# Graph attention: one-hot matrices of edges by one VectorE compare per step, six PSUM banks for the sums, and a reordered seam between edge stage and node stage

## What is computed

```
def _gat_layer(x, src, dst, W, a_src, a_dst, b, heads, concat):
    n = x.shape[0]
    h = (x @ W).reshape(n, heads, -1)
    al_s = jnp.einsum('nhf,hf->nh', h, a_src)
    al_d = jnp.einsum('nhf,hf->nh', h, a_dst)
    e = jax.nn.leaky_relu(al_s[src] + al_d[dst], NEG_SLOPE)
    m = jax.lax.stop_gradient(jax.ops.segment_max(e, dst, num_segments=n))
    ex = jnp.exp(e - m[dst])
    denom = jax.ops.segment_sum(ex, dst, num_segments=n)
    alpha = ex / (denom[dst] + 1e-16)
    out = jax.ops.segment_sum(h[src] * alpha[:, :, None], dst, num_segments=n)
    out = out.reshape(n, -1) if concat else out.mean(axis=1)
    return out + b
```

## Time and profile before

| | before |
|---|---|
| median of 3 timed runs | 7338.19 us (7330.99 to 7347.03) |
| the profiled execution | 7389.03 us |
| its span in the trace | 7387.3 us |
| mean granted TensorE clock | 0.754 |
| TensorE busy | 4888.9 us, 66% |
| VectorE busy | 4342.4 us, 59% |
| GpSimd busy | 3668.7 us, 50% |
| ScalarE busy | 2620.5 us, 35% |

### The profile page before, as it was taken

How to read it: one execution, slowest core, us unless ns; L and a number is a source line. 1 busy time by engine, 2 the same in 40 slices (tenths; PEclk the granted TensorE clock), 3 DMA queues, 4 the chain that set the end, 5 groups by cost and what they waited for, 6 DMA issues and landing times. The chain is left out here.

```text
span 7387.3 us, 99572 instructions
## 1 busy us (share of the span) xinstructions
PE 4888.9 (66%) x21954; PEld 3578.6 (48%) x21954; DVE 4342.4 (59%) x12539; ACT 2620.5 (35%) x7524; POOL 3668.7 (50%) x3680
## 2 busy tenths in 40 slices
PE   5666699996666666666666667466666666666662
PEld 4455488885444444444444445344444444444441
DVE  8999776665455555545555558444444454544447
ACT  6774222221444444444444445222222222222221
POOL 1333311112566666666666653566666666666660
PEclk8887799997666767676777779676667776777676
DMA  8999644333343434343444334333333333333336
GB/s 341 378 390 384 244 126 136 110 110 96 107 116 111 116 112 115 111 114 112 116 111 115 111 101 132 108 110 111 106 110 105 109 105 111 105 110 105 110 110 224
DMA packets 384742, 1062.90 MB, mean 144 GB/s; under 512 B 103698, under 2 KB 195782, under 8 KB 359382
## 3 DMA queue, kind: packets, MB, share of 16 engines
q0 software_dynamic: 168928, 459.50, 23.4%
q1 hardware_dynamic: 206902, 549.39, 20.5%
q10 hardware_dynamic: 8640, 51.39, 1.7%
HBM read 795.11 MB, written 264.87 MB: 143 GB/s over the span
## 5 line engine op out<-in xcount | busy, mean ns | idle before, releaser
L259 POOL DMA_INDIRECT rows<-table_d,idx x3328 | 3215.4, 966 | 2095.4 <-issue 801.6
L307 PE MATMUL pG<-rows,onehot 128*128 128x264 f32 (+1 forms) x6656 | 2568.1, 537 | 934.0 <-issue 660.3
L510 DVE TENSOR_TENSOR acc<-acc,pG 128x264 f32 (+1 forms) x3328 | 1413.8, 425 | 1898.8 <-remote 743.0
L307 PEld LDWEIGHTS pG<-rows,onehot 128*128 128x128 f32 x6656 | 1625.9, 264 | 1516.2 <-issue 885.5
L371 ACT ACTIVATE onehot<-pQ 128x1024 f32<-128x1024 f32 (+1 forms) x512 | 439.7, 859 | 2515.0 <-DMA pre_in<-pre_d 1347.5
L378 ACT ACTIVATE rows<-rows 128x64 f32<-128x64 f32 (+1 forms) x4480 | 1255.4, 367 | 26.9 <-issue 22.4
L938 PE MATMUL pH<-hT_pre,w1h 128*128 128x256 f32 x1568 | 470.5, 466 | 188.6 <-ACT hT_pre L799 150.0
L938 PEld LDWEIGHTS pH<-hT_pre,w1h 128*128 128x128 f32 x1568 | 366.0, 240 | 277.2 <-ACT hT_pre L799 166.4
L1075 DVE SCALAR_TENSOR_TENSOR run<-run,same_e,ea 128x96 f32<-128x96 f32 x1567 | 488.5, 312 | 7.2 <-DMA ea<-in_ea 6.3
L1075 DVE SCALAR_TENSOR_TENSOR run<-run,cut_e,ea 128x96 f32<-128x96 f32 x1567 | 488.3, 312 | 0.0
L492 DVE TENSOR_TENSOR rows<-rows,pA 128x1024 f32<-128x1024 f32 x384 | 466.9, 1216 | 4.4
(11 more groups left out here) (295 smaller groups left out, 4560.5 us busy)
## 6 DMA issues: line engine op xcount, KB each, us to landing
rows_d<-run SPq DMA_DIRECT2D x98, 1536.0 KB
onehotT<-drow_d SPq DMA_DIRECT2D x128, 832.0 KB
ea<-in_ea SPq DMA_DIRECT2D x98, 768.0 KB
rows<-table_d,idx POOLq DMA_INDIRECT x3328
pre_d<-pre ACTq DMA_DIRECT2D x49, 1024.0 KB
pre_in<-pre_d SPq DMA_DIRECT2D x49, 1024.0 KB, 5.1
hrow_c<-table_d SPq DMA_DIRECT2D x98, 256.0 KB
tab<-tab_d SPq DMA_DIRECT2D x64, 260.0 KB
```

Source lines behind the costliest of these rows:

```text
L259: g.indirect_dma_start(out=rows[:, at.par, k, 0:XF + H], out_offset=None, in_=table, in_offset=bass.IndirectOffsetOnAxis(ap=idx[:, at.par, ...
L307: mm = pe.matmul(pG[(k + 2 * at.par) % 4][:, 0:W], onehot[:, k, :], rows[:, at.par, k, :], start=True, stop=True)
L510: v.tensor_tensor(to, to, pG[(k + 2 * at.par) % 4][:, 0:W], ALU.add).then_inc(added, 1)
```

## The change

In attention, `spans`, `hots`, the tiles drow and pQ, the loads of drow and the semaphores between them are gone. In their place `edge_hots` on VectorE compares a row of 128 numbers (`keep["iota"]`) with a table of each edge's place in its node tile (`keep["near"]`, 128 x 1664 in bf16, made once in `node_mlp` and kept in SBUF): one instruction per step for 26 items, in the order late items of b, early items of b+1. The aggregates have six banks instead of four. ScalarE weighs the late items in one run. The DRAM array drow has one row instead of five.

At the seam, the places where runs begin are computed between groups of edges (`heads_of_runs`, three groups behind `ROW_AT`); the last group's run is stored in two halves; the scatter is awaited by GpSimd at the start of `node_mlp`; the weights have semaphores of their own, those of attention are issued by ScalarE; TensorE waits only for w1, and `project_attention` stands behind step 0 and step 16. The item tables lose some VectorE operations, and a third list (near, 13 tiles) is transposed in steps 14 to 17.

```
 attention
+            def edge_hots(b, first=False, chain=True):
+                w = EARLY if first else TB if chain else TB - EARLY
+                near = keep["near"][:, 0:w] if first else keep["near"][:, bass.ds(b.n * TB + EARLY, w)]
+                i = TB - w if first else 0
+                v.tensor_tensor(onehot[:, i:i + w, :], keep["iota"][:, :].unsqueeze(1).to_broadcast([P, w, P]),
+                                near.unsqueeze(2).to_broadcast([P, w, P]), ALU.is_equal).then_inc(edges_hot, 1)
...
             def step(b, first=False, chain=True, ahead=True, after=True):
                 n = b.plus(1)
+                edge_hots(b, first, chain)
                 if not first:
                     late = node_tiles(nc, v, jrow_v, b, EARLY, TB)
...
             def aggregate(at, ks):
                 for k in ks:
-                    if k % QT == 0:
-                        pe.wait_ge(near_used, near_at(at, k // QT) + 1)
+                    if k == 0:
+                        pe.wait_ge(edges_hot, at.n + 1)
+                    if k == EARLY:
+                        pe.wait_ge(edges_hot, at.n + 2)
...
                     if k % 2 == 0:
-                        pe.wait_ge(added, at.n * TB + (k + 2))
-                    mm = pe.matmul(pG[(k + 2 * at.par) % 4][:, 0:W], onehot[:, k, :], rows[:, at.par, k, :],
+                        bank_read = k - BANKS + 2 if k >= BANKS else k - BANKS if k else 0
+                        pe.wait_ge(added, at.n * TB + (BANKS + bank_read))
+                    mm = pe.matmul(pG[k % BANKS][:, 0:W], onehot[:, (k - EARLY) % TB, :], rows[:, at.par, k, :],
                                    start=True, stop=True)
...
                 part(EARLY, 16)
-                spans(n, 0, first)
...
-                spans(n, 2)
                 if ahead:
                     destinations(m, tiles)
-                aggregate(n, range(0, 8))
-                spans(n, 3)
-                aggregate(n, range(8, EARLY))
+                aggregate(n, range(0, EARLY))
...
-                hots(n, 0)
-                hots(n, 1)
...
-                weigh(n, range(EARLY, 16))
-                hots(n, 2)
-                weigh(n, range(16, 20))
-                hots(n, 3)
-                weigh(n, range(20, TB))
+                weigh(n, range(EARLY, TB))
...
-                if after:
-                    sp.wait_ge(near_ready, near_at(n, NQ - 1) + 1)
-                    load_drow(o)
...
 edge_chains, node_mlp
-        assert ROW_AT < NG and PAIR == 2 and EW <= ET
+        HEADS_AT = ROW_AT + 3
+        assert HEADS_AT < NG and PAIR == 2 and EW <= ET
...
+                if g == HEADS_AT:
+                    heads_of_runs()
...
-            g.wait_ge(fix_out, 16)
...
+            g.wait_ge(keep["fix_out"], 16)
             all_steps(g, step, first=0)
...
-            pe.wait_ge(w_in, 16 * 10)
-            pe.wait_ge(projected, 1)
+            pe.wait_ge(w1_in, 16 * 5)
...
-            v.wait_ge(w_in, 16 * 10)
-            project_attention(v, chain, wg, att, tmp, H)
-            v.sem_inc(projected, 1)
...
                 if n == 0:
-                    v.wait_ge(late_in, 16 * 4)
+                    v.wait_ge(wg_in, 16 * 3)
+                    project_attention(v, chain, wg, att, tmp, H)
+                    v.sem_inc(projected, 1)
+                if n == 16:
+                    v.wait_ge(late_in, 16 * 3)
                     project_attention(v, chain, wg2, att2, tmp, 1)
```

More of the change, by code:

```diff
@@ L117, in attention @@
     D = XF // H
-    QT = 8
-    CHUNKS = [range(q, min(q + QT, TB)) for q in range(0, TB, QT)]
-    NQ = len(CHUNKS)
     EARLY = 12
+    BANKS = 6
     DG = EARLY // 4
@@ L241, in _ @@
             load_jv(one)
-            sp.wait_ge(blank, 1)
-            load_drow(one)
-            load_drow(two)
             load_jpe(two)
@@ L272, in _ @@
         def _(pe):
-            def spans(at, q, first=False):
-                if q == 0:
-                    pe.wait_ge(drow_in[at.par], at.fills * 16 + 16)
-                if not first:
-                    pe.wait_ge(near_used, near_at(at, q))
-                for k in CHUNKS[q]:
-                    mm = pe.matmul(pQ[:, k - q * QT, :], drow[:, at.par, k, :], keep["nrow"][:, :],
-                                   start=True, stop=True, skip_group_check=True)
-                mm.then_inc(near_ready, 1)
             def destinations(at, tiles):
@@ L1040, in tile_row, with heads_of_runs @@
                 done(v.tensor_copy(keep["jT"][:, :], pU[1][0:KT, 0:P]))
+            def heads_of_runs():
+                v.wait_ge(counted, 2)
+                v.scalar_tensor_tensor(out=place[:, 1:EW], in0=same[:, 1:EW], scalar=float(EW), in1=count_i[:, 1:EW],
+                                       op0=ALU.mult, op1=ALU.add).then_inc(masked, 1)
+                v.wait_ge(masked, 6)
+                v.memset(place[:, 0:1], float(EW)).then_inc(masked, 1)
+                v.wait_ge(masked, 7)
+                v.tensor_reduce(head[:, :], place[:, :], AX.X, ALU.min).then_inc(masked, 1)
+                v.wait_ge(masked, 8)
+                v.tensor_scalar(whole[:, 0:1], head[:, :], float(EW), None, ALU.is_ge).then_inc(masked, 1)
+                v.scalar_tensor_tensor(out=head[:, :], in0=head[:, :], scalar=float(EW), in1=first_i[:, :],
+                                       op0=ALU.min, op1=ALU.add).then_inc(masked, 1)
+                v.wait_ge(masked, 10)
+                v.tensor_copy(head_i[:, :], head[:, :]).then_inc(heads, 1)
+                v.tensor_tensor(whole[:, 0:1], whole[:, 0:1], same[:, 0:1], ALU.mult).then_inc(masked, 1)
+                v.wait_ge(masked, 11)
+                v.tensor_scalar(whole[:, 1:2], whole[:, 0:1], -1.0, BIG, ALU.add, ALU.mult).then_inc(masked, 1)
+                v.wait_ge(masked, 12)
+                for m in range(2):
+                    v.tensor_copy(wide[:, m, :], whole[:, m:m + 1].to_broadcast([P, EF])).then_inc(masked, 1)
+                v.wait_ge(masked, 14)
+                v.sem_inc(heads, 1)
             def between(g):
@@ L1612, in lists_copied @@
                     v.wait_ge(list_turned, turned_by(n))
-                    v.tensor_copy((keep["last"], src)[q][:, k0 * P:(k0 + w) * P], pF0[:, 0:w * P]).then_inc(list_copied, 1)
+                    v.tensor_copy((keep["last"], src, keep["near"])[q][:, k0 * P:(k0 + w) * P], pF0[:, 0:w * P]).then_inc(list_copied, 1)
                 if n == TURN_ENDS:
@@ L1617, in lists_copied @@
                     done(v.tensor_copy(lastsT[:, :, :], pF[0:KT, 0:3, :]))
-                    done(v.tensor_copy(keep["nrow"][0:5, :], pF[0:5, 3, :]))
                     v.sem_inc(list_copied, 1)
```

164 lines of the change are left out of this document (65 added, 99 removed).

## The result

| | before | after |
|---|---|---|
| median of 3 timed runs | 7338.19 us | 7458.98 us (7453.19 to 7465.32) |
| ratio | | 1.0159, 95% interval 1.0144 to 1.0173 |
| span in the trace | 7387.3 us | 7451.4 us |

The changed kernel is 121 us slower. I had forecast 7250 us, in a range of 7070 to 7420, with 29% on slower: the time lies above the range, and the sign is the other one.

A forecast was written before the change was run, and what follows sets the result against it. Attention, three quarters of the program, was taken as a cycle of waits with no full engine. Terms 45 - 42 - 64 - 16 - 15 + 3.5 = -89 us, from the median 7338.2, gave 7250 us, range 7070 to 7420.

The forecast's parts named there:

- the hold: Attention: the compare delaying GpSimd's gathers; counted as nothing, since 31.5 + 3.75 = 35.3 us stays below the 40.97 us step.
- rival E: Attention: the compare holds GpSimd's gathers, costing half of 3.75 us in 128 steps, 240 us: 7490 us; chance 4%.
- The compare: New VectorE instruction in each attention step, between item 11's sum and the register load: 3.75 us long.
- The gap between the sums of items 11 and 12: On VectorE, must hold compare and product, 5.9 us; 1.5 us too short at 30 four-head loop edges: +45 us.
- rival A: Attention: the compare lies on the path, item 12 3.75 us late in all 60 loop-edge steps: 7470 us; chance 17%.
- The load of node one-hots: SyncE in attention: issued some 10 us earlier, saving 1.4 us in 30 steps: -42 us.
- Late completions: Attention: idle spells named remote come from SyncE's loads and vanish, 2 us a step: 6990 us; chance 13%.
- TensorE's 26 products: Small products dropped from each attention step; 0.5 us saved in each of 128 steps: -64 us.
- rival B: TensorE in attention: less work lowers the mean clock from 0.70 to 0.65, slower, say 7370 us; chance 11%.
- Six banks: Attention's sums with six banks, not four: 0.25 us saved in 64 steps, -16 us.
- The seam: Before attention: first transposes of features come earlier, -15 us; 13 transposes added to a full TensorE, +3.5 us.

The follow-up runs named there:

- slow condition: Groups of runs in which the kernel before took 7341 to 7388 us, near the 7338 of the first timing.
- quick condition: Groups of runs in which the kernel before took 6432 and 6434 us.
- r5: The kernel before, unchanged, run for a profile in the group of e12, slow condition; its attention took 5385.7 us.
- e12: Changed kernel with the compare's row of 128 numbers copied to PSUM, slow condition: 0.9983 of the kernel before.
- e11: Changed kernel with the row in PSUM, four banks, compare split in two, late half ahead of the loop edge: 1.0036 of the kernel before, slow condition.
- e8: Changed kernel with the compare's row in PSUM, the same kernel as e12, in the quick condition: 1.0354 of the kernel before.
- e7: Kernel before with SyncE's load of drow moved behind load_jv, so node one-hots are sent for first: 1.0025 of the kernel before, slow condition.
- e5: Kernel before with only the seam of the changed kernel: 0.9998 of the kernel before, slow condition.

## Why the prediction was wrong

**The step that failed** is the hold, which the forecast's sum put at nothing: "31.5 + 3.75 = 35.3 us would still be below 40.97". It stands in rival E, with the mechanism and a price, 7490 us against 7459 measured, at 4%. That the price is so near is luck: it takes half of 3.75 us a step, where 1.0 was measured, and adds it to 7249, where the kernel without the hold is at about 7326. Two readings made the rival so small. First, I took L867's median of 1.07 us beside a busy VectorE as a sign that VectorE does not hold gathers. The median hid the long ones: 29 of these 98 gathers take from 2.0 us up to the row's greatest value, 8.04. The trace of the kernel before has this at one of them:

```profile
303.47 0.31 DVE L1075 SCALAR_TENSOR_TENSOR run<-run,cut_e,ea 128x96 f32<-128x96 f32 x1
303.53 5.66 POOL L867 DMA_INDIRECT k_lists<-in_dst,full_i  x1 [0.30 <-issue]
...
308.06 0.32 DVE L1075 SCALAR_TENSOR_TENSOR run<-run,cut_e,ea 128x96 f32<-128x96 f32 x1
```

VectorE runs L1075, with two inputs in SBUF, without a pause, and the gather ends 0.8 us behind the last of them, as behind the compare. At most other long ones VectorE goes on when the gather ends. 69 gathers pass beside the same instructions in at most 1.08 us. No run tests what parts the two kinds, but gathers of up to 8 us beside VectorE were there to be read.

Second, I took GpSimd's 9 us of waits a step as cover. Of the hold's 2.9 us a step they covered 1.9 in the slow condition, and not all: by the order in the traces, what GpSimd waits for at the end of a step is released 2.5 us after its own last gather, so that a late gather delays its own release. In the quick condition the changed kernel has hardly any such waits left.

The Trainium skill ("SBUF — State Buffer", SBUF: two separate sides) gave the rule that decided: an instruction of VectorE with two SBUF inputs and one of GpSimd that reads SBUF exclude each other for the whole length. The trace agrees for a gather that starts inside the compare (3.67 us beside a compare of 3.63, and 0.95 once one input is in PSUM), but not for one that is already running: it and the compare overlap, and neither gets longer. The same page of the Trainium skill (Who interferes with whom) infers that such a tensor_tensor leaves the writing of DMA descriptors alone. The indirect DMA was held all the same; it also reads its indices from SBUF, and the runs don't tell which of its two parts was held.

**The compare** at 3.75 us: measured 3.62. The gap between the sums of items 11 and 12: I needed 5.9 us; with 1 head it is 6.07 (6020.51 to 6026.58). At the loop edges with 4 heads I was wrong: in the medians the gap grew from 5.4 us (7.5 in r5) to 9.7, more than the 1.5 that I took, and 3.64 us named issue stand ahead of the compare, not beside it. In the slow condition this cost nothing that shows: e12 has the same gaps (9.8 us) at 0.9983, and e11's shorter ones bring nothing. So there rival A is not what happened, although TensorE's waits name the compare more than anything else (474.6 us in 60 steps). In the quick condition it is not excluded: e8 has the gap of 9.7 us too, and is 3.5% above the kernel before.

**The load of node one-hots** (-42 us) is refuted in the slow condition by e7: +18 us. **Late completions** did vanish ahead of items 10 and 11, as I had said (6.49 us of remote before, none at 3016), and came back ahead of item 22 (9.38 us). The cause that I named, SyncE's loads, was argued from nearness in time only, and e7 speaks against it.

**TensorE's 26 products and the clock.** The mean clock in attention fell from 0.70 to 0.67, as rival B feared, but e12 has 0.67 too and is as fast as the kernel before, so the fall costs no more than the rest of the change gave. No run tells the -64 us apart from it.

**Six banks** -16 us: about -30 where it was measured, in the quick condition. **The seam** -11.5 in sum: -1.5 for e5, whose interval (-9 to +6) just excludes the forecast.

So of -89 us predicted, what stands in the slow condition without the hold is -12 us (e12, -5 to -20), and the hold added some 130.

## What to carry to other kernels

Before a long VectorE instruction with both inputs in SBUF goes beside GpSimd's indirect DMAs, price it twice: once as work on VectorE, once as a gather that lasts as long; if one input is small and constant, put it in PSUM. The wait time of an engine is cover only if what it waits for doesn't depend on its own last instruction, which the traces here suggest and don't prove. And a wait that names a new instruction isn't its cost: in the slow condition the compare with 474.6 us of waits to its name could stay as long as it was, and 1.8% lay in a queue that no wait named. A median says nothing about a hold; read the greatest value and how many are near it.

The best version in the slow condition is e12, the changed kernel with the row in PSUM, 0.9983 of the kernel before; in the quick condition the kernel before is the best that was measured (e8 is at 1.0354). What the remaining 3.5% there are made of stays open. One candidate is the gap at the loop edges with 4 heads, which no run shortened there without touching something else.

## What the runs showed of the hardware

- A gather (an indirect DMA of 128 rows, issued on GpSimd) that started inside a compare with two SBUF inputs took 3.81 us in the median of 129, not 0.95, and ended 0.82 us behind the compare. With one input in PSUM it stayed at 0.95 (369 gathers); the compare took 3.62 us either way. A gather that was running when the compare started kept its 0.95.
- The compare of onehotT, 1.08 us with one SBUF input, does the same in the kernel before: 115 gathers start inside one and take 1.38 us in the median, ending 0.81 us behind it.
- The kernel before took 6432 to 6434 us in two groups of runs and 7338 to 7388 in the others, with one chip in both. e8 and e12, one kernel in both conditions, have the same gather pace (967 ns). Their traces differ in the mean granted clock (0.755 and 0.730) and in when TensorE's completions are seen: with 1 head the sums of items 18 and 19 start 1.2 us behind the end of their products in e8 and 6.5 in e12, in the median. Which pair is late changes with the kernel: in the changed one it is items 22 and 23, 7.7 us in the median, seen 2.5 us after GpSimd's last gather. That the gathers cause it was not tested: no run takes them away. Why a group falls in one condition or the other is not known.
